# Four adjacency layers on one core: the first pass of layer 3 in the seven-product form too, and layer 2's chain laid out in half units

## The chip, the cores and the metric

The kernel runs on one NeuronCore of a Trainium2 chip, as one launch. The metric is the device time of that launch in microseconds. TensorE (PE in the profile) multiplies, VectorE (DVE), ScalarE (ACT) and GpSimd (POOL) do the elementwise work, and SyncE (SP) issues the DMAs. The median of three runs of the kernel before is 1045.57 us (1045.5 to 1046.95).

## The reference

Four layers share one 2048 x 2048 matrix `adj` (a sparse 0/1 pattern with a full diagonal, each row divided by its sum) and x of 8 batches x 2048 nodes x 64 channels. After each layer stands a residual and a layer norm. Cut to what matters:

```python
x = layernorm(x + L0(x, adj))        # x, A x and (2 A A - I) x, each by weights of its node
x = layernorm(x + L1(x, adj))        # attention over adj > 0.5
# layer 2
adj_i = adj + eye(N); deg = sum(adj_i, axis=1)
x = layernorm(x + (adj_i @ (x @ W.T + b)) / deg)
# layer 3: three passes, with node 0 set to intervention_value first
v = x.at[:, 0].set(intervention_value)
for _ in range(3):
    effects = adj @ v
    h = relu(concat([v, effects]) @ W1.T + b1)
    v = h @ W2.T + b2
x = layernorm(x + v)
```

## The kernel before

**Storage.** The 512 columns (8 batches x 64) form four chunks c = 0 to 3 of 128 columns. The 2048 nodes form four blocks j = 0 to 3 of 512 nodes. The pattern of `adj` lies in SBUF in fp8 (`Bm`, in the buffer `BW`), the row scales apart from it. Each moving operand x or v is held in `S` as a sum of two fp16 halves (high and low), so a product costs two matmuls for each of the 16 tiles of 128 nodes.

**Plain products.** A step P(k), k = 0 to 15, is layer 2's product for one (c, j): 32 matmuls of 512 columns in four pieces of 8 (`quarter`), and 8 of 128 columns with the diagonal. P(16) to P(31) are the first of layer 3's three passes: 32 matmuls of 512 columns and 3 more (`beside`), which add the part of W1 that multiplies v. The results go to the PSUM banks 0, 1, 2 in turn, and the step E(k) takes them out.

**Seven-product form.** The second and third pass take two chunks at once (n = 4 to 7; n // 2 is the pass, n % 2 the pair of chunks). Matrix and operand are cut into two by two blocks, and seven products of blocks do for eight, after a scheme of Winograd's kind. A product is a slot s = 0 to 6. Its operand is a block of v (X11, X12, X22) or a sum of blocks (S1 to S4). Its matrix block is a quarter of the pattern or a combination (T1 to T4, which GpSimd makes in the 64 steps `bt`). A slot is run in two half steps of 16 matmuls of 512 columns (jj = 0, 1). `V(n, s, jj)` takes a half step's bank out: ScalarE copies for s = 0 and 2, VectorE adds for s = 1, 3, 4, 5, and splits finished results into high and low half. `G` multiplies h by W2 and the adjacency weights, 12 matmuls of 128 columns. `mix` makes S1 to S4 on VectorE, `cut` splits an operand into its two halves, on ScalarE and then on GpSimd.

**Scales.** The fp16 halves need scales. For the second and third pass they are measured: VectorE takes the largest value of each block (a reduction to `gm` in `high`), a matmul (`gcol`) brings it across partitions, and the step `step` works out the next scale from it.

**Layer 2's chain.** Between P(4c+3) and layer 3's use of chunk c stands a chain over all engines, each step once for each j: W (TensorE by weights, then VectorE adds to X), `sq` (ScalarE) and `red` (VectorE) for the variance, `var`, a root on ScalarE, `rs` (five small VectorE instructions, the first of which is the reciprocal), `apply` (VectorE, X times 1/std), `v0t` and `v0` (ScalarE makes the high half of v in `S`, VectorE the low one), D (TensorE by the diagonal; ScalarE and VectorE split it into T), and G. `chk` and `sgn` (ScalarE, 16 each) check the matrix beside all this.

**Order.** Every engine runs one list in order, written out ahead by hand. `middle_order` lays the layers 0 and 1, `last_order` everything from P(1) on. In `last_order` a table puts each step ahead of a P(k) (one unit: about 8 us on TensorE) or a half step h of the seven-product part. All engines walk the same list and take from it what is theirs, and semaphores keep them apart. So the distance in the list between the maker and the user of a value is the time that it may take.

**Banks.** W, D, G, F take PSUM banks in rotation. `take_banks` works out for each such step, and for each half step that opens a bank (`pair_free`), what must have emptied that bank; TensorE waits for it. `D` on TensorE also waits for VectorE's last part of `v0` (`s_vl`). Lines of the steps: P L889, M L931, D L964, G L969, E on VectorE L1548, V on VectorE L1560, W on VectorE L1601, v0 L1620. In the profile the VectorE helpers `stt`, `ts`, `red` give L1224, L1216 or L1217, and L1227, apply is L1528, and mix L1600.

## Time and profile before

| | us |
|---|---|
| median of 3 runs | 1045.57 |
| profiled execution | 1046.92 |
| its span, first to last instruction | 1045.1 |
| TensorE busy | 1024.1 |
| VectorE busy | 692.9 |
| GpSimd busy | 534.7 |
| ScalarE busy | 453.1 |
| mean granted clock of TensorE | 0.995 of full |

The profile shows one execution. Its own time is 1.82 us above its span, and 1.35 us above the median. Busy time is time in which an engine has an instruction in work; matmuls overlap, so a matmul's mean duration is longer than the distance from one to the next. Layer 2 and the first pass of layer 3 lie between 525 and 792 us from the start of the span, the other two passes behind.

### The profile page before, as it was taken

How to read it: one execution, taken by the hardware profiler on the slowest of the kernel's cores; microseconds unless marked ns; L12 is line 12 of the kernel's file. 1: busy time of each engine (PE TensorE's matmuls, PEld its weight loads, DVE VectorE, ACT ScalarE, POOL GpSimd, SP SyncE). 2: the span in 40 equal slices, each digit the busy share in tenths (PEclk: the TensorE clock that was granted, in tenths of full speed). 3: DMA queues.
4: the chain of work that ended last, by engine and by line, in shares of the span. 5: the costliest groups of instructions: out<-in, count | busy, mean ns of one | idle time of the engine just before them, and what ended most of it. 6: DMA issues, size and time to landing. Idle time of an engine off the chain costs nothing.

```text
span 1045.1 us, 18762 instructions
## 1 busy us (share of the span) xinstructions
PE 1024.1 (98%) x6922; PEld 492.3 (47%) x6922; DVE 692.9 (66%) x1728; ACT 453.1 (43%) x1097; POOL 534.7 (51%) x625
## 2 busy tenths in 40 slices
PE   7999999999999999999999999999999999999995
PEld 3445444444444444434455555555554545455553
DVE  4877565656555886686577777875546676767556
ACT  4632323333334543444424667556557622141632
POOL 0005486644546686577645758579764233223311
PEclk9999999999999999999999999999999999999998
DMA  9930000000000000000010121112212100000022
GB/s 369 400 129 1 2 1 2 1 2 2 1 1 2 2 1 2 1 1 2 1 41 2 41 82 51 71 41 82 81 42 82 41 1 1 3 1 22 21 61 61
DMA packets 14658, 45.66 MB, mean 44 GB/s; under 512 B 960, under 2 KB 9280, under 8 KB 10080
## 3 DMA queue, kind: packets, MB, share of 16 engines
q1 hardware_dynamic: 14560, 44.39, 11.5%
q8 instruction: 57, 0.93, 0.4%
q14 instruction: 41, 0.34, 0.1%
HBM read 40.19 MB, written 4.19 MB: 42 GB/s over the span
## 4 chain that ended last, share of the span: by engine, by line
PE 95%; DVE 3%; ACT 1%; issue 0%; DMA 0%; SPq 0%; DVEq 0%; ACTq 0%
PE PS L771 37%; PE PS L901 23%; PE PS L945 18%; PE PS L823 5%; PE PS L756 2%; PE PS L758 2%; PE PS L757 2%; PE PS L765 1%; PE PS L764 1%; PE PS L763 1%; PE PS L746 1%; PE PS L926 1%; PE PS L747 1%; DVE X L1224 1%; DVE T L1224 0%; PE PS L809 0%
## 5 line engine op out<-in xcount | busy, mean ns | idle before, releaser
L771 PE MATMUL PS<-BW,S 128*128 128x512 fp8e4 x1792 | 403.2, 379 | 0.8 <-DVE R L1224 0.8
L771 PEld LDWEIGHTS PS<-BW,S 128*128 128x128 f16 x1792 | 169.9, 98 | 207.3 <-issue 16.6
L1064 ACT ACTIVATE T<-PS,SM 128x128 f32<-128x128 f32 x384 | 112.8, 365 | 234.5 <-DVE X L1224 157.2
L901 PE MATMUL PS<-WZ,R 64*128 64x512 f16 x1536 | 198.0, 377 | 1.7 <-ACT T L1064 1.7
L1768 POOL TENSOR_TENSOR T<-T 128x128 f32<-128x128 f32 (+1 forms) x192 | 124.3, 648 | 127.8 <-ACT T L1064 117.5
L1224 DVE SCALAR_TENSOR_TENSOR X<-PS,SM,X 128x128 f32<-128x128 f32 x320 | 110.0, 344 | 81.9 <-PE PS L901 81.9
L901 PEld LDWEIGHTS PS<-WZ,R 64*128 64x128 f16 x1536 | 69.5, 94 | 104.6 <-issue 26.3
L945 PE MATMUL PS<-BW,S 128*128 128x512 fp8e4 x512 | 115.4, 379 | 0.3 <-issue 0.3
L1224 DVE SCALAR_TENSOR_TENSOR T<-PS,SM,T 128x128 f32<-128x128 f32 x256 | 88.2, 344 | 28.9 <-PE PS L901 28.6
L1768 POOL TENSOR_TENSOR S<-R,S 128x512 f16<-128x512 f32 x48 | 57.5, 1210 | 93.5 <-ACT S L1064 93.5
L901 PE MATMUL PS<-WZ,T 64*128 64x512 f16 x768 | 103.8, 376 | 0.0
L1768 POOL TENSOR_TENSOR T<-R,T 128x512 f16<-128x512 f32 x42 | 49.6, 1187 | 75.4 <-DVE T L1216 52.7
L1790 POOL TENSOR_TENSOR BW<-BW 128x512 fp8e4<-128x512 fp8e4 x64 | 75.6, 1207 | 0.0
L945 PEld LDWEIGHTS PS<-BW,S 128*128 128x128 f16 x512 | 49.2, 98 | 55.7 <-issue 0.7
L1064 ACT ACTIVATE R<-PS,cs 128x512 f32<-128x512 f32 x48 | 32.7, 681 | 98.0 <-PE PS L765 68.7
L945 PE MATMUL PS<-BW,T 128*128 128x512 fp8e4 x320 | 72.8, 379 | 0.0
L1064 ACT ACTIVATE WZ<-WZ,ra 128x2048 f16<-128x2048 f32 (+1 forms) x32 | 63.9, 1996 | 0.5
L1768 POOL TENSOR_TENSOR X<-X,T 128x128 f32<-128x128 f32 x128 | 58.5, 457 | 10.0
L1216 DVE TENSOR_SCALAR T<-R 128x512 f16<-128x512 f32 x48 | 31.5, 657 | 47.5 <-ACT R L1064 46.6
L823 PE MATMUL PS<-BW,S 128*128 128x512 fp8e4 x240 | 54.9, 394 | 5.7 <-DVE BW L1221 5.7
L756 PE MATMUL PS<-hat,T 128*128 128x128 f16 x320 | 57.1, 220 | 2.4 <-DVE T L1224 2.4
L901 PEld LDWEIGHTS PS<-WZ,T 64*128 64x128 f16 x768 | 37.4, 94 | 45.5
(215 smaller groups left out, 1480.0 us busy)
## 6 DMA issues: line engine op xcount, KB each, us to landing
WZ<-a_in SPq DMA_DIRECT2D x16, 1024.0 KB, 4.8
BW<-at_in SPq DMA_DIRECT2D x8, 1024.0 KB, 18.5
R<-at_in SPq DMA_DIRECT2D x7, 1024.0 KB, 12.4
out<-X SPq DMA_DIRECT2D x16, 256.0 KB, 2.3
X<-x_in SPq DMA_DIRECT2D x3, 1024.0 KB, 19.9
T<-w_in SPq DMA_DIRECT2D x1, 1536.0 KB, 15.4
R<-at_in SPq DMA_DIRECT2D x2, 512.0 KB, 4.8
SM<-sm_in SPq DMA_DIRECT2D x1, 520.5 KB, 18.0
```

Of the source, the lines that this page charges most:

```text
L756: e.matmul(ok, th, hat[:, 0, kind, :], start=True, stop=False)
L757: e.matmul(ok, tl, hat[:, 0, kind, :], start=False, stop=False)
L758: m = e.matmul(ok, th, hat[:, 1, kind, :], start=False, stop=True)
L771: m = e.matmul(o, stile(h, t, c), Bm[:, t, block(j)], start=(t == 0 and h == 0), stop=(last and t == NT - 1 and h == 1))
L823: e.matmul(bank(2 * c + j), stile(h, jt, c), Bm[:, jt, block(j)], start=(jt == 0 and h == 0), stop=False)
L901: m = e.matmul(bank(b0 + q), halves[kd][zh][r, :], WZ[r, wh, kd, block(g)], start=(i == 0), stop=(i == 8))
L945: m = e.matmul(o, half_of(n, what, h, q % 2)[:, t, :], b[:, 4 * (q % 2) + t, :], start=(s in (0, 1, 3) and q % 2 == 0 and t == 0 and h == ...
L1064: return e.activation(o, i, f, **kw)
L1216: return e.tensor_scalar(o, i, s1, None, o1)
L1224: return e.scalar_tensor_tensor(out=o, in0=a, scalar=s, in1=b, op0=f, op1=g)
L1768: return e.tensor_tensor(o, a, b, f)
L1790: e.tensor_tensor(o, a, b, f, saturate=False).then_inc(s_bt, 1)
```

## The change

All three passes of layer 3 now have the seven-product form: n = 2 and 3 take the place of P(16) to P(31). The combinations of the matrix are needed earlier and in the order T3, T2, T1, T4, so GpSimd's `bt` steps start at P(1) and not at P(8). The scales of all passes are worked out beforehand from bounds, in `scales_b`; `gmax`, `gcol`, `step` and the reductions to `gm` are gone. Layer 2's chain is placed by half units y (a P(k) is two of them, y = 2k and 2k + 1; from y = 32 on y is the half step y - 32), and closer: D(c, 0) stands two half units behind `v0(c, 0)`, where it stood two units behind. The block E of the first pass is gone, with its VectorE and GpSimd parts. Some operands of n = 2 and 3 lie in a buffer in SM, and the squares of layer 2 in part of BW.

```diff
+BT_ORDER = ("T3", "T2", "T1", "T4")
...
-    return 16 * (p - 1) + (4 * c + j if p == 1 else 8 * (c // 2) + PAIR_UNITS.index((c % 2, j)))
+    return 16 * (p - 1) + 8 * (c // 2) + PAIR_UNITS.index((c % 2, j))
...
+    late, half, between = {}, {}, {}
+    def at(y, *steps):
+        (late if y < 32 else half).setdefault(y if y < 32 else y - 32, []).extend(steps)
+    def on(h, *steps):
+        half.setdefault(h, []).extend(steps)
 
     for k in sorted(after):
-        at(k, *after[k])
+        at(2 * k, *after[k])
     for c in range(NC):
         for j in range(4):
-            at(4 * c + j + 3, ("W", c, j))
-            at(4 * c + j + 4, ("sq", 2, c, j), ("red", 2, c, j))
-        k = 4 * c + 7
-        at(k, ("var", 2, c))
-        at(k + 1, ("rs", 2, c), ("apply", 2, c, 0), ("apply", 2, c, 1), ("v0t", c))
-        at(k + 2, ("apply", 2, c, 2), ("apply", 2, c, 3), ("v0", c, 0), ("v0", c, 1))
-        at(k + 3, ("v0", c, 2), ("v0", c, 3))
-        at(k + 4, ("D", c, 0), ("D", c, 1))
-        at(k + 5, ("D", c, 2), ("D", c, 3))
-        at(k + 6, ("G", 1, c, 0), ("G", 1, c, 1))
-        at(k + 7, ("G", 1, c, 2), ("G", 1, c, 3))
-    at(4, ("rows",))
+            y = 2 * (4 * c + j)
+            at(y + 4, ("W", c, j))
+            at(y + (5 if c == 3 else 6), ("sq", 2, c, j), ("red", 2, c, j))
+        y = 8 * c + (12 if c == 3 else 13)
+        at(y, ("var", 2, c))
+        at(y + 1, ("rs", 2, c), ("apply", 2, c, 0), ("apply", 2, c, 1), ("v0t", c))
+        at(y + 2, ("apply", 2, c, 2), ("apply", 2, c, 3), ("v0", c, 0), ("v0", c, 1))
+        at(y + 3, ("v0", c, 2), ("v0", c, 3))
+        at(y + 4, ("D", c, 0), ("D", c, 1))
+        at(y + 5, ("D", c, 2), ("D", c, 3))
+    at(8, ("rows",))
     for it in range(NT):
-        at(6 + 2 * it, ("chk", it))
-        at(7 + 2 * it, ("sgn", it))
-    at(24, ("gmax", 1, 0))
-    at(25, ("gcol", 1, 0), ("step", 1, 0))
-    at(27, *take(4, 0, "X11", "X12"))
-    at(28, cut(4, 0, "X11"), cut(4, 0, "X12"), *take(4, 0, "X21", "X22"))
-    at(29, *mixes(4, 0, 1, 3, 2), cut(4, 0, "X22"), cut(4, 0, "S2"), *mixes(4, 0, 4), *take(4, 1, "X11", "X22"))
-    at(30, cut(4, 0, "S1"), cut(4, 0, "S3"), cut(4, 0, "S4"), cut(4, 1, "X11"), cut(4, 1, "X22"), *take(4, 1, "X12", "X21"))
-    at(31, *mixes(4, 1, 1, 3, 2), cut(4, 1, "X12"), cut(4, 1, "S2"), *mixes(4, 1, 4))
+        at(12 + 4 * it if it < 5 else 32 + 4 * (it - 5) - (it - 5) // 4, ("chk", it))
+        at(14 + 4 * it if it < 5 else 34 + 4 * (it - 5) - (it - 5) // 4, ("sgn", it))
     for i in range(64):
-        at(8 + i // 3, ("bt", i))
-    for k in range(32):
-        order += late.pop(k, []) + (pieces("P", k) + [("E", k)] if k else [])
-    half = {}
-    def on(h, *steps):
-        half.setdefault(h, []).extend(steps)
-    for k in sorted(late):
-        on(2 * (k - 32), *late[k])
-    on(1, cut(4, 1, "S1"))
-    on(2, cut(4, 1, "S3"), cut(4, 1, "S4"))
-    for n in (5, 6, 7):
-        h, (p, g) = 14 * (n - 5), divmod(n - 2, 2)
-        on(h, ("gmax", p, g))
-        on(h + 2, ("gcol", p, g), ("step", p, g), *take(n, 0, "X11"))
+        at(2 + 4 * i // 7 if i < 56 else 38 + (i - 56) // 2, ("bt", i))
+    for n, y in ((2, 20), (3, 37)):
+        at(y, *take(n, 0, "X11", "X12"))
+        at(y + 1, cut(n, 0, "X11"), *take(n, 1, "X11", "X12"), cut(n, 0, "X12"))
+        at(y + 2, cut(n, 1, "X11"), cut(n, 1, "X12"))
+    for n, y in ((2, 28), (3, 43)):
+        at(y, *take(n, 0, "X21", "X22"))
+        at(y + 1, *mixes(n, 0, 1, 3, 2), cut(n, 0, "X22"), cut(n, 0, "S2"))
+        at(y + 2, cut(n, 0, "S3"), *mixes(n, 0, 4), *take(n, 1, "X22"), cut(n, 0, "S1"))
+        at(y + 3, cut(n, 0, "S4"), *take(n, 1, "X21"))
+        at(y + 4, *mixes(n, 1, 1, 3, 2), cut(n, 1, "X22"), cut(n, 1, "S2"))
+        at(y + 5, *mixes(n, 1, 4), cut(n, 1, "S1"))
+        at(y + 6, cut(n, 1, "S3"), cut(n, 1, "S4"))
+    for k in range(16):
+        p = pieces("P", k)
+        order += late.pop(2 * k, []) + (p[0:2] if k else []) + late.pop(2 * k + 1, []) + (p[2:4] + [("E", k)] if k else [])
+    for n in (4, 5, 6, 7):
+        h = 14 * (n - 3)
...
+    on(44, ("flags",))
+    on(46, ("total",))
+    on(47, ("verdict",))
...
-            n, s, jj = 4 + h // 14, h % 14 // 2, h % 2
+        if h < 84:
+            n, s, jj = 2 + h // 14, h % 14 // 2, h % 2
...
-        SQC = [flatR[:, 4096 + 512 * k:4608 + 512 * k] for k in range(2)] + [rowt[:, 512 * k:512 * k + 512] for k in range(2)]
+        SQC = [BW[:, NT * N + 28672 + 2048 * k:NT * N + 30720 + 2048 * k].bitcast(F32) for k in range(2)] + [rowt[:, 512 * k:512 * k + 512] for k in range(2)]
...
+        def made(n, jj, what):
+            return XB[:, 0 if what == "X11" else 1, :] if apart(n, jj, what) else MADE[what]
+        def apart(n, jj, what):
+            return n < 4 and jj == 1 and what in ("X11", "X12", "S4")
...
-                            for k in range(30, 32) if m == 4 else ():
-                                held[product_bank(k)] = (s_gt, k - 15)
-                            if m == 4:
-                                held[2] = (s_gt, 14)
+                            for k in range(13, 16) if m == 2 else ():
+                                held[product_bank(k)] = (s_zl, k + 1)
...
-                    if p == 0:
-                        e.wait_ge(s_sl, 4 * c + q + 1)
-                    else:
-                        e.wait_ge(s_ul, CN["G", p, c, q] + 1)
+                    e.wait_ge(s_sl, 4 * c + q + 1)
...
-                    if n == 4 and s == 2:
-                        e.wait_ge(s_bt, 64)
+                    if n == 2 and by[0] == "T":
+                        e.wait_ge(s_bt, NT * (1 + BT_ORDER.index(by)))
...
-                            m = beside(e, o, *ending(n, s, jj), 1, on=s > 1)
+                            m = beside(e, o, *ending(n, s, jj), min(n // 2 - 1, 1), on=s > 1)
...
-                elif kind == "gcol":
-                    p, g = step[1:]
-                    o = pe_aux(e, step)
-                    e.wait_ge(s_gmx, 2 * (p - 1) + g + 1)
-                    e.matmul(o[:, 0:128], gmh[:, g:g + 1].broadcast_to([128, 128]), i16[:, :], start=True,
-                             stop=True).then_inc(s_gmc, 1)
...
-                        fn(RT[k % 4], bank(product_bank(k)), ACT.Relu, scale=col(cKG0)).then_inc(s_gt, 1)
...
-                        e.wait_ge(s_p, 16 + 4 * block_of(n, jj, "X21" if what == "S4" else what)[0] + 4)
-                    fn(half_of(n, what, 0, jj), four(MADE[what]), ACT.Copy).then_inc(s_uh, 1)
+                        c, j = block_of(n, jj, "X21" if what == "S4" else what)
+                        e.wait_ge(s_d, 4 * c + j + 1)
+                    fn(half_of(n, what, 0, jj), four(made(n, jj, what)), ACT.Copy).then_inc(s_uh, 1)
...
-                fc(ts(e, col(cHB), col(cHB), 1e-10, qmax, ALU.max, ALU.mult))
-                fc(ts(e, col(cHB), col(cHB), 1.0 / 30000, None, ALU.mult))
-                fc(e.reciprocal(col(cT2), col(cHB)))
-                fc(ts(e, col(cKG0), col(cT2), col(cIRho), col(cT0), ALU.mult, ALU.mult))
-                fc(ts(e, cs[:, cSG:cSG + 4], ones[:, 0:4], col(cT2), None, ALU.mult))
-                fc(ts(e, cs[:, cISG:cISG + 4], ones[:, 0:4], col(cHB), None, ALU.mult))
+                fc(ts(e, col(cHB), col(cHB), 1e-10, None, ALU.max))
+                fc(e.tensor_tensor(col(cNMG), cs[:, cNG + 1:cNG + 2], cs[:, cNM + 1:cNM + 2], ALU.add))
+                fc(ts(e, col(cNMG), col(cNMG), 1e-3, None, ALU.max))
+                ip, sp, kp = ([col(k + p) for p in range(4)] for k in (cISG, cSG, cKG))
+                for p in (1, 2, 3):
+                    if p > 1:
+                        fc(stt(e, col(cHB), col(cHB), col(cNMG), col(cC1), ALU.mult, ALU.add))
+                    fc(ts(e, ip[p], col(cHB), qmax, 1.0 / (12000 if p < 3 else 60000), ALU.mult, ALU.mult))
+                    fc(e.reciprocal(sp[p], ip[p]))
+                    fc(ts(e, kp[p], sp[p], col(cIRho + min(p - 1, 1)), ip[p - 1] if p > 1 else col(cT0), ALU.mult, ALU.mult))
...
-            def high(f, c, j, n, largest):
-                hi = T[:, c, 0, block(j)]
-                ts(e, hi, f, 0.0, None, ALU.max).then_inc(s_gh, 1)
-                if largest:
-                    e.wait_ge(s_gh, n + 1)
-                    red(e, gm[:, c, j:j + 1], hi, ALU.max).then_inc(s_gm, 1)
...
+                ts(e, T[:, c, 0, block(j)], f, 0.0, None, ALU.max).then_inc(s_gh, 1)
...
-                        high(RT[k % 4], c, j, k - 16, True)
...
-                elif kind == "gmax":
-                    p, g = step[1:]
-                    e.wait_ge(s_gm, 16 * (p - 1) + 8 * g + 8)
-                    red(e, gmh[:, g:g + 1], gm[:, 2 * g:2 * g + 2, :].rearrange("p c j -> p (c j)"), ALU.max).then_inc(s_gmx, 1)
-                elif kind == "step":
-                    p, g = step[1:]
-                    sG, iG = cs[:, cSG + g:cSG + g + 1], cs[:, cISG + g:cISG + g + 1]
-                    n = 2 * (p - 1) + g + 1
-                    e.wait_ge(s_gmc, n)
-                    red(e, gmr[:, g:g + 1], bank(aux_bank["gcol", p, g])[:, 0:128], ALU.max).then_inc(s_gmr, 1)
-                    e.wait_ge(s_gmr, n)
-                    fc(e.tensor_tensor(col(cT0), gmr[:, g:g + 1], iG, ALU.mult))
-                    fc(e.tensor_tensor(col(cT1), col(cT0), col(cIQ), ALU.mult))
-                    fc(ts(e, col(cT1), col(cT1), col(cNG + 1), col(cC1), ALU.mult, ALU.add))
-                    fc(ts(e, col(cT1), col(cT1), fr[:, 1:2], None, ALU.mult))
-                    fc(stt(e, col(cT0), col(cT0), col(cNM + 1), col(cT1), ALU.mult, ALU.add))
-                    fc(ts(e, col(cT0), col(cT0), 1e-10, 1.0 / 15000, ALU.max, ALU.mult))
-                    fc(ts(e, CR[:, g, :], c1row[:, :], sG, col(cRho + 1), ALU.mult, ALU.mult))
-                    fc(e.reciprocal(sG, col(cT0)))
-                    fc(ts(e, cs[:, cKG + g:cKG + g + 1], sG, iG, col(cIRho + 1), ALU.mult, ALU.mult))
-                    e.tensor_copy(iG, col(cT0)).then_inc(s_kg, 1)
-                    e.wait_ge(s_kg, n)
...
+                    if k == 3 and q == 8:
+                        e.wait_ge(s_red, REDN[2, NC - 1, 3] + 1)
...
-                    add(T[:, c, 1, block(j)], RT[k % 4], T[:, c, 0, block(j)], ALU.subtract).then_inc(s_gl, 1)
```

What stands on the engines then, at the places that the prediction speaks of:

TensorE ahead of chunk 0's first D, before: P(10) ends (L926), and D (L746) follows it. The wait for s_vl is the one for `v0`.

```order
L771 MATMUL PS<-BW,S 128x512 [waits s_sl]
L771 MATMUL PS<-BW,S 128x512 x7
L771 MATMUL PS<-BW,S 128x512 [waits s_sl]
L771 MATMUL PS<-BW,S 128x512 x7
L926 MATMUL PS<-dg,S 128x128 x8
L746 MATMUL PS<-dg,S 128x128 [waits s_vl,s_y2]
```

TensorE after, at the same place: this is the middle of P(8), and its second half follows the two D.

```order
L769 MATMUL PS<-BW,S 128x512 [waits s_sl,s_zl]
L769 MATMUL PS<-BW,S 128x512 x7
L769 MATMUL PS<-BW,S 128x512 [waits s_sl]
L769 MATMUL PS<-BW,S 128x512 x7
L744 MATMUL PS<-dg,S 128x128 [waits s_vl,s_msum]
```

D(0, 0) has moved from behind P(10) into P(8), two and a half units earlier in TensorE's list.

VectorE ahead of layer 3, before, chunk 2's `apply` (L1528) and `v0` (S<-R and S<-X) with W(3, 2) (X<-PS) behind them:

```order
L1528 TENSOR_TENSOR X<-X,T 128x4x128 [waits s_rs] x2
L1224 SCALAR_TENSOR_TENSOR S<-R,cs,S 128x128 [waits s_vh]
L1224 SCALAR_TENSOR_TENSOR S<-X,cs,S 128x3x128
L1224 SCALAR_TENSOR_TENSOR S<-X,cs,S 128x4x128 [waits s_vh]
L1227 TENSOR_REDUCE T<-R 128x8 [waits s_sq]
L1224 SCALAR_TENSOR_TENSOR X<-PS,ra,X 128x128 [waits s_sc,s_bl,s_w]
L1224 SCALAR_TENSOR_TENSOR X<-PS,ra,X 128x128 x3
```

VectorE after, the same, from the second pair of `apply` to W(3, 2); R<-PS is a G, T<-PS is E(15):

```order
L1503 TENSOR_TENSOR X<-X,T 128x4x128 [waits s_rs] x2
L1198 SCALAR_TENSOR_TENSOR S<-R,cs,S 128x128 [waits s_vh]
L1198 SCALAR_TENSOR_TENSOR S<-X,cs,S 128x3x128
L1198 SCALAR_TENSOR_TENSOR S<-X,cs,S 128x4x128 [waits s_vh]
L1201 TENSOR_REDUCE T<-BW 128x8 [waits s_sq]
L1198 SCALAR_TENSOR_TENSOR R<-PS,ra,R 128x128 [waits s_ul,s_g]
L1198 SCALAR_TENSOR_TENSOR R<-PS,ra,R 128x128 x3
L1198 SCALAR_TENSOR_TENSOR T<-PS,T 128x512 [waits s_zh]
L1198 SCALAR_TENSOR_TENSOR S<-X,cs,S 128x4x128 [waits s_vh] x2
L1198 SCALAR_TENSOR_TENSOR X<-PS,ra,X 128x128 [waits s_sc,s_bl,s_w]
L1198 SCALAR_TENSOR_TENSOR X<-PS,ra,X 128x128 x3
```

All four `v0` of chunk 2 and E(15) now stand ahead of W(3, 2).

TensorE at the start of layer 3, before: a G or W (its last matmul is L758), and then P(16).

```order
L758 MATMUL PS<-hat,T 128x128
L771 MATMUL PS<-BW,S 128x512 [waits s_ul,s_zl]
L771 MATMUL PS<-BW,S 128x512 x7
L771 MATMUL PS<-BW,S 128x512 [waits s_ul]
```

TensorE after: W(3, 2) ends (L756), and the first half step of n = 2 follows, in the bank 4 that W(3, 2) has just written.

```order
L756 MATMUL PS<-hat,T 128x128
L936 MATMUL PS<-BW,S 128x512 [waits s_ul,s_y2]
L936 MATMUL PS<-BW,S 128x512 x7
L936 MATMUL PS<-BW,S 128x512 [waits s_ul]
L936 MATMUL PS<-BW,S 128x512 x7
L744 MATMUL PS<-dg,S 128x128 [waits s_vl,s_y2]
```

`s_y2` counts VectorE's W: the half step waits for VectorE's part of the W ahead of it (`held[4]` in `take_banks` is `(s_y2, 15)`, the fifteenth W).

## Rows read from the trace of the kernel before

**Rows 1.** The page's line of busy time, share and instructions.

```profile
PE 1024.1 (98%) x6922; PEld 492.3 (47%) x6922; DVE 692.9 (66%) x1728; ACT 453.1 (43%) x1097; POOL 534.7 (51%) x625
```

**Rows 2.** Page, chain that ended last: shares by engine.

```profile
PE 95%; DVE 3%; ACT 1%; issue 0%; DMA 0%; SPq 0%; DVEq 0%; ACTq 0%
```

**Rows 3.** Busy time by stretch: PE, PEld, DVE, ACT, POOL, clock, DMA, GB/s.

```profile
651.00:721.00 70.00, 70.00 (x470) 37.59 (x468) 57.74 (x102) 44.12 (x62) 50.73 (x42) 1.00 0.18 61
792.00:851.00 59.00, 59.00 (x347) 29.75 (x346) 40.05 (x83) 30.84 (x41) 19.44 (x16) 1.00 0.12 45
```

**Rows 4.** Chain in order of time: start, us, what; P(8) and P(9).

```profile
582.03 6.91 PE PS L771 x32
588.94 0.45 PE PS L926 x8
590.06 6.91 PE PS L771 x32
```

**Rows 5.** Groups, 514 to 911 us, by form: count, busy us, mean ns, idle before.

```profile
L1528 DVE TENSOR_TENSOR X<-X,T 128x512 f32<-128x512 f32 x28 | 29.0, 1075 | 0.2
L1224 DVE SCALAR_TENSOR_TENSOR T<-PS,T 128x512 f16<-128x512 f32 x32 | 20.9, 684 | 21.4 <-ACT T L1064 21.3
L1600 DVE TENSOR_TENSOR R<-R 128x512 f32<-128x512 f32 x24 | 19.5, 835 | 3.4 <-POOL S L1768 2.3
L1224 DVE SCALAR_TENSOR_TENSOR S<-X,cs,S 128x512 f16<-128x512 f32 x12 | 15.9, 1352 | 3.9 <-ACT S L1064 3.9
L1224 DVE SCALAR_TENSOR_TENSOR S<-X,cs,S 128x384 f16<-128x384 f32 x4 | 4.9, 1236 | 0.0
L1224 DVE SCALAR_TENSOR_TENSOR S<-R,cs,S 128x128 f16<-128x128 f32 x4 | 3.9, 969 | 0.0
L1224 DVE SCALAR_TENSOR_TENSOR R<-X,cs,R 128x128 f32<-128x128 f32 x4 | 2.2, 553 | 0.0
L1064 ACT ACTIVATE T<-PS 128x512 f16<-128x512 f32 x32 | 17.5, 586 | 13.0 <-PE PS L926 12.9
```

**Rows 6.** VectorE in order of time: start, us, instruction; chunks 0, 2 and 3.

```profile
576.83 3.46 DVE L1528 TENSOR_TENSOR X<-X,T 128x512 f32<-128x512 f32 x4
...
582.48 1.12 DVE L1224 SCALAR_TENSOR_TENSOR X<-PS,ra,X 128x128 f32<-128x128 f32 x4
...
653.38 0.34 DVE L1518 RECIPROCAL T<-T 128x32 f32<-128x32 f32 x1
...
655.72 1.29 DVE L1528 TENSOR_TENSOR X<-X,T 128x512 f32<-128x512 f32 x2
...
661.85 2.15 DVE L1224 SCALAR_TENSOR_TENSOR R<-PS,ra,R 128x128 f32<-128x128 f32 x8
663.91 3.06 DVE L1528 TENSOR_TENSOR X<-X,T 128x512 f32<-128x512 f32 x2
...
692.97 0.34 DVE L1518 RECIPROCAL T<-T 128x32 f32<-128x32 f32 x1
...
697.01 2.12 DVE L1528 TENSOR_TENSOR X<-X,T 128x512 f32<-128x512 f32 x2
```

**Rows 7.** GpSimd in order of time.

```profile
652.00 3.19 POOL L1790 TENSOR_TENSOR BW<-BW 128x512 fp8e4<-128x512 fp8e4 x3
661.29 1.16 POOL L1768 TENSOR_TENSOR T<-R,T 128x512 f16<-128x512 f32 x1 [6.11 <-DVE T L1216]
663.71 2.72 POOL L1768 TENSOR_TENSOR S<-R,S 128x512 f16<-128x512 f32 x2 [1.26 <-ACT S L1064]
```

**Rows 8.** TensorE in order of time: a gap near the end.

```profile
1035.36 0.22 PE L756 MATMUL PS<-hat,T 128*128 128x128 f16 x1 [2.06 <-DVE T L1224]
1035.41 0.22 PE L757 MATMUL PS<-hat,T 128*128 128x128 f16 x1
...
1035.94 0.31 PE L758 MATMUL PS<-hat,T 128*128 128x128 f16 x1
1036.05 0.31 PE L756 MATMUL PS<-hat,T 128*128 128x128 f16 x1
```

203 lines of the change are left out of this document (80 added, 123 removed).

## The prediction

> **What bounds the kernel now.** I read the line of busy time first: TensorE is busy for 1024.1 of 1045.1 us, VectorE for 692.9 [rows 1]. Then the chain that ended last: 95% of it is TensorE [rows 2]. So a matmul taken out counts in full, as long as no other engine makes TensorE wait for longer than that. Then the stretches, because a mean over the span hides where the others are near. From 651 to 721 us, at the start of layer 3, VectorE is busy for 57.74 of 70.00 us, though TensorE never waits there. Later, from 792 to 851 us, where n = 4 and 5 run, it is busy for 40.05 of 59.00 [rows 3]. The change puts the seven-product form into the first of these two stretches. That is why I follow VectorE's queue, and last look at single instructions in order of time [rows 6, 7].
>
> **What goes on TensorE.** P(16) to P(31) are 16 x 32 = 512 matmuls of 512 columns. The 28 half steps of n = 2 and 3 are 28 x 16 = 448. The 48 matmuls of `beside`, G, W and D stay. 32 such matmuls take 6.91 us, 0.216 us each [rows 4], so 64 fewer save 13.8 us. Four small matmuls of `gcol` go too. The trace shows no stall around them; I count 0.2 us. Gain: 14.0 us.
>
> **What it adds on VectorE.** The 16 blocks E of the first pass go with their reductions. V and `mix` for two n come: 16 mixes of 0.835 us alone are 13.4 us [rows 5]. V has three additions with splits and one addition for each n and jj, and that is more than E had. Of the 70 us from 651 on VectorE had 12.3 us free; the same work now has some 7 us less of TensorE time beside it. Layer 2's chain is drawn closer as well. A mean load near 1 is no wait in itself. What counts is where TensorE needs VectorE's newest result. I find four such places. Durations are the means of rows 5 where a row is named by kind; `rs` is five instructions from 653.38 to 655.72, 2.34 us; the four instructions of a W are 1.12 us, those of a G 2.15 / 2 = 1.07 us [rows 6]. A reduction of 512 elements is taken like VectorE's part of E, 0.68 us. TensorE's side is made of 6.91 us for 32 matmuls, 0.45 us for the eight with the diagonal, and 590.06 - 589.39 = 0.67 us for a W or G [rows 4].
>
> *Place 1, D(0, 0) and D(0, 1), now in the middle of P(8).* Before the change layer 1's last `apply` ends at 576.83 + 3.46 = 580.29 us [rows 6]. Now chunk 0's chain stands right behind it: rs 2.34, two apply 2.15, v0t 0.55, red 0.68, W 1.12, two apply 2.15, v0(0, 0) 0.97 + 1.24, v0(0, 1) 1.35. The sum is 12.55, so v0(0, 0) is there at 591.5 and v0(0, 1) at 592.8. P(8) starts at 582.03 [rows 4] plus one W more, and half of it is over at 586.2. TensorE waits for 5.3 us and then for 0.9 us: 6.2 us. If everything runs in 0.6 of its mean, as the pair of apply at 655.72 does (1.29 for 2.15), about 1 us is left. With rs at 4.04 (692.97 to 697.01) and pairs of apply at 3.06 [rows 6] it is 9.7.
>
> *Place 2, D(1, 0) and D(1, 1) in P(12).* Counted from the end of P(10): E(10) 0.59 + 0.68 on two engines, then the same 12.55: 13.8 us. TensorE has W, P(11), W, half of P(12) and D(1, 0) ahead of D(1, 1): 12.6 us. Wait: 1.2 us, from 0 to 5.
>
> *Place 3, the first half step of n = 2.* It takes bank 4, which W(3, 2) has written just ahead of it, so it waits for VectorE's part of W(3, 2) (`s_y2`). On VectorE that part stands behind nearly all of chunk 2's chain. From the end of P(14): E(14) 1.27, rs 2.34, two apply 2.15, v0t 0.55, W 1.12, mix 0.84, G 1.07, two apply 2.15, v0(2, 0) 2.21, v0(2, 1) 1.35, red 0.68, G 1.07, E(15) 0.68, two v0 2.70, W(3, 2) 1.12: 21.3 us. TensorE has four W or G and P(15), 2.7 + 7.4 = 10.0 us. Wait: 11.3 us. Even with VectorE free until P(15) ends, E(15), two v0 and W come behind it: 1.27 + 2.70 + 1.12 - 0.67 = 4.4 us. So 4 is the low end. With the slow durations of place 1 the high end is 15.5. Before the change no such wait was possible: P(16) took the bank of a product that had ended two units earlier.
>
> *Place 4, D(3, j) in n = 2.* Counted from the end of place 3's wait, VectorE has caught up. v0(3, 0) and G(1, 2, 3), whose banks D(3, 0) and D(3, 1) need, are ready within about 1 us of the time TensorE asks for them. I take 0, up to 5. The later half steps stand as n = 4 to 7 do, which ran with VectorE two thirds busy: 0.
>
> *The clock.* After a gap of 2.06 us near the end of the span the 128-column matmuls go from a distance of 0.05 us to 0.11 us [rows 8]: the granted clock falls from 2.4 to 1.2 GHz. Places 1 and 3 are longer gaps. How soon the clock comes back this trace doesn't show. If 16 matmuls of 512 columns run at half rate, 3.45 us are lost; if none, nothing. I take 1.5 us for each of the two gaps, 3.0 in all, between 0 and 6.9. The Trainium skill ("TensorE: Matmul & The Clock Gate", Part 1) says that the throttled state is the default and that sustained activity releases it, which speaks for a cost above zero at both gaps; by a rule that a warm array stays warm the term would be 0. The first half of it agrees with the row, the way back is shown by no row here.
>
> **Other edits.** `bt` starts earlier: 64 instructions, 56 of them beside layer 2. M with T2 needs 32, with T1 48, with T4 64 of them, and they stand two or more half steps ahead: no wait. `scales_b` has a few more one-column instructions at P(1), where VectorE has a slack of units. `chk` and `sgn` move on ScalarE, which was busy for 44.12 of 70 us. I cost these at nothing; ScalarE's and GpSimd's idle time hides them.
>
> **Sum.** Waits 6.2 + 1.2 + 11.3 + 0 + 3.0 = 21.7 us, gain 14.0 us, net +7.7 us. The profiled execution of 1046.92 us becomes 1054.6 us; it stood 1.35 us above the median, so the median goes from 1045.57 to 1053.3 us.
>
> **Rivals.**
> 1. *VectorE is quick, and the change is a gain.* The durations above are long because GpSimd works beside them. With GpSimd idle, from 655.19 to 661.29 us, two apply take 1.29 us; with it at work, from 663.71 on, 3.06 us [rows 6, 7]. If GpSimd has its pauses where the chain runs, the waits are 1 + 0 + 4 + 0, with no clock lost: 5 us against 14.0. Time: 1036.6 us. It decides at place 3: under a wait of some 6 us there, the sum of the waits stays under the gain. Against it: `bt` now stands in those pauses.
> 2. *GpSimd slows VectorE everywhere.* GpSimd was busy for 50.73 of 70 us already [rows 3], and 56 of the 64 `bt` now fall into the 16 units of layer 2, where 24 stood. With rs at 4.04 and pairs at 3.06 each time the waits are 9.7 + 4 + 15.5 + 3, with 5 for the clock: 37 us. Time: 1068.6 us. The Trainium skill ("GPSIMD Engine Reference", 1. Specifications) lists contention of GpSimd with VectorE instructions that have two SBUF inputs; by that rule every apply and v0 beside `bt` is slow, and the sum would be this one. The trace agrees for the pair at 663.91 us and shows that without GpSimd it is gone.
> 3. *The waits just eat the gain.* Places 1 and 3 at 4 and 8, 2 us elsewhere: 14 us, 1045.6 us.
> 4. *The change doesn't do what it says*, because the list makes TensorE wait for `cut` of n = 2, not for the bank. ScalarE and GpSimd finish those for X11 seven units ahead; S2 has five half steps. I give it nothing of its own; its price would be in 3.
>
> **How the numbers follow.** The forecast (some 4 us around the sum) has 0.48, rival 1 with its way to the forecast 0.27, rival 2 0.19, rival 3 0.06. A difference of 0.2%, 2.1 us, is about what can be told from none. Faster by more: 0.27; within: 0.06; slower: 0.67. The range from 1036 to 1064 us takes in rival 1 and the lower half of rival 2; the likeliest case's own range is 1048 to 1060.
>
> **What would show it.** Right: TensorE idle at the D of chunk 0 and ahead of the first half step of n = 2, with VectorE as releaser (5 and 11 us); a granted clock below 1 right behind; 64 fewer matmuls of 512 columns. Wrong: TensorE's chain without a gap between 525 and 800 us, or gaps that wait for GpSimd or ScalarE; VectorE's pairs of apply near 1.3 us there.

## The result and the profile after

The changed kernel takes 1071.05 us (median of 4 runs, 1070.51 to 1071.63), the kernel before 1045.53 on the same chip: the ratio is 1.024, with an interval from 1.0226 to 1.0254. The prediction said 1053.3, range 1036 to 1064. The direction was right, the size was not, and the time lies outside the range. The profiled execution's span is 1069.3 us; before it was 1045.1.

The page's line of busy time and the chain by engine of the changed kernel, beside [rows 1, 2]:

```profile
PE 1015.5 (95%) x6854; PEld 487.6 (46%) x6854; DVE 693.1 (65%) x1701; ACT 459.4 (43%) x1109; POOL 540.5 (51%) x625
```

```profile
PE 83%; DVE 8%; issue 4%; POOL 2%; ACT 2%; DMA 0%; SPq 0%; POOLq 0%; DVEq 0%; ACTq 0%
```

The 68 matmuls are gone (6922 to 6854). VectorE is as busy as before (693.1 against 692.9 us), but it now has 8% of the chain, and "issue" 4%. The waits themselves are TensorE's only gaps over 0.4 us from 500 to 760 us (start, duration, instruction, idle time before it and what ended it):

```profile
549.49 0.27 PE L754 MATMUL PS<-hat,T 128*128 128x128 f16 x1 [9.06 <-issue]
...
610.09 0.27 PE L744 MATMUL PS<-dg,S 128*128 128x128 f16 x1 [13.56 <-DVE S L1198]
...
611.59 0.26 PE L744 MATMUL PS<-dg,S 128*128 128x128 f16 x1 [0.49 <-DVE S L1198]
...
692.02 5.78 PE L936 MATMUL PS<-BW,S 128*128 128x512 fp8e4 x16 [9.65 <-DVE X L1198]
```

The reader is to see three places. The second and third are D(0, 0) with D(0, 1) and the first half step of n = 2, places 1 and 3 of the prediction. The first is W(0, 1) ahead of P(3), and the prediction doesn't have it. The profile names no releaser for that first wait ("issue"); what TensorE waited for is read from VectorE's rows below. The last row also shows the clock: its 16 matmuls of 512 columns take 5.78 us, and the next 16, with the clock up, take 3.62:

```profile
698.53 3.62 PE L936 MATMUL PS<-BW,S 128*128 128x512 fp8e4 x16
```

Busy time by stretch (PE, PEld, DVE, ACT, POOL, clock, DMA, GB/s), within the gaps and right after them:

```profile
540.00:550.00 10.00, 0.94 (x14) 0.79 (x12) 8.99 (x31) 0.00 (x0) 4.30 (x5) 0.64 0.00 1
550.00:560.00 10.00, 10.00 (x62) 5.37 (x61) 5.21 (x15) 2.83 (x5) 7.78 (x7) 0.85 0.01 2
600.00:610.00 10.00, 0.00 (x0) 0.00 (x0) 10.00 (x13) 5.39 (x10) 9.92 (x8) 0.54 0.27 105
610.00:613.00 3.00, 2.42 (x18) 1.91 (x19) 3.00 (x4) 1.66 (x4) 3.00 (x3) 0.50 0.04 8
692.00:695.00 3.00, 2.98 (x8) 1.05 (x9) 1.85 (x3) 0.63 (x1) 0.27 (x1) 0.50 0.00 0
```

From 600 to 610 us TensorE does nothing while VectorE is busy for all 10 us and GpSimd for 9.92. The sum: 1045.1 - 14.0 for the matmuls + 9.1 + 14.0 + 9.7 of waits makes 1063.9; the 5.4 us that are left to the measured 1069.3 I put down to the lower clock behind the three gaps. TensorE's busy time says the same: 1015.5 us, where 1024.1 - 14.0 would be 1010.1.

VectorE in order of time, ahead of the first wait. E(1)'s low half, which W(0, 1) needs, is the last row; it ends at 549.38, and W(0, 1) starts at 549.49:

```profile
539.09 1.02 DVE L1369 TENSOR_TENSOR cs<-cs 128x1 f32<-128x1 f32 x1
...
541.20 1.02 DVE L1198 SCALAR_TENSOR_TENSOR cs<-cs 128x1 f32<-128x1 f32 x1
542.25 1.02 DVE L1375 TENSOR_TENSOR cs<-cs 128x1 f32<-128x1 f32 x1
...
545.30 0.22 DVE L1198 SCALAR_TENSOR_TENSOR cs<-cs 128x1 f32<-128x1 f32 x1
...
548.69 0.69 DVE L1198 SCALAR_TENSOR_TENSOR T<-PS,T 128x512 f16<-128x512 f32 x1
```

GpSimd there:

```profile
540.06 4.25 POOL L1739 TENSOR_TENSOR BW<-BW 128x512 fp8e4<-128x512 fp8e4 x4
```

`scales_b` runs from 538.72 to 547.47 us, 8.75 us; before, it was done in 4.3 (539.29 to 543.63), and E(1)'s low half stood here:

```profile
544.86 0.69 DVE L1224 SCALAR_TENSOR_TENSOR T<-PS,T 128x512 f16<-128x512 f32 x1
```

Part of the growth is instructions, part is this: the same one-column instruction takes 1.02 us while GpSimd's four `bt` run (540.06 to 544.31) and 0.22 us a microsecond after them. (The first row's 1.02 us is no growth: it stands beside another GpSimd instruction and took 1.03 before, at 539.67.) And W(0, 1) stands one unit earlier than it did, so TensorE asked at 540.4 for what it had asked for at 548.2. Had E(1) been ready as early as before, at 545.55, TensorE would still have waited 5 us.

The chain between layer 1's last apply, which ends at 594.88, and D(0, 0):

```profile
595.17 0.88 DVE L1494 TENSOR_TENSOR T<-T 128x32 f32<-128x32 f32 x1
596.09 1.07 DVE L1495 TENSOR_TENSOR T<-T 128x32 f32<-128x32 f32 x1
597.20 1.29 DVE L1191 TENSOR_SCALAR T<-T 128x32 f32<-128x32 f32 x1
598.52 1.09 DVE L1497 TENSOR_TENSOR T<-T 128x32 f32<-128x32 f32 x1
599.65 2.36 DVE L1503 TENSOR_TENSOR X<-X,T 128x512 f32<-128x512 f32 x2
...
604.72 2.75 DVE L1503 TENSOR_TENSOR X<-X,T 128x512 f32<-128x512 f32 x2
607.39 1.18 DVE L1198 SCALAR_TENSOR_TENSOR S<-R,cs,S 128x128 f16<-128x128 f32 x1
608.49 2.95 DVE L1198 SCALAR_TENSOR_TENSOR S<-X,cs,S 128x384 f16<-128x384 f32 x2
```

These are the slow durations of the mean and above (rs 4.8 us, pairs of apply 2.36 and 2.75, against 3.06 at 663.91 in [rows 6]): 15.2 us to D(0, 0), where I had 11.2 to v0(0, 0).

### The profile page after: what moved, and what is told of

Same layout as the page of the kernel before. It is cut to its first block, busy times and chain, and to the rows that moved or that the text cites. A ratio compares the mean times of both kernels' runs of the same rounds, so it can differ in the third digit from the quotient of the medians.

```text
span 1069.3 us, 18663 instructions
## 1 busy us (share of the span) xinstructions
PE 1015.5 (95%) x6854; PEld 487.6 (46%) x6854; DVE 693.1 (65%) x1701; ACT 459.4 (43%) x1109; POOL 540.5 (51%) x625
## 3 DMA queue, kind: packets, MB, share of 16 engines
q1 hardware_dynamic: 14560, 44.39, 11.3%
## 4 chain that ended last, share of the span: by engine, by line
PE 83%; DVE 8%; issue 4%; POOL 2%; ACT 2%; DMA 0%; SPq 0%; POOLq 0%; DVEq 0%; ACTq 0%
PE PS L936 27%; PE PS L899 22%; PE PS L769 19%; PE PS L821 5%; PE PS L754 1%; PE PS L755 1%; PE PS L756 1%; DVE X L1503 1%; DVE R L1198 1%; PE PS L763 1%; PE PS L762 1%; PE PS L761 1%; DVE X L1198 1%; DVE S L1198 1%; DVE T L1198 1%
## 5 line engine op out<-in xcount | busy, mean ns | idle before, releaser
L769 PE MATMUL PS<-BW,S 128*128 128x512 fp8e4 x1280 | 293.0, 381 | 0.8 <-DVE R L1198 0.8
L769 PEld LDWEIGHTS PS<-BW,S 128*128 128x128 f16 x1280 | 120.8, 98 | 151.3 <-issue 19.9
L936 PE MATMUL PS<-BW,S 128*128 128x512 fp8e4 x768 | 175.3, 382 | 10.0 <-DVE X L1198 9.7
L936 PEld LDWEIGHTS PS<-BW,S 128*128 128x128 f16 x768 | 74.3, 99 | 95.0 <-DVE X L1198 9.8
L936 PE MATMUL PS<-BW,T 128*128 128x512 fp8e4 x480 | 109.3, 379 | 0.0
L1715 POOL TENSOR_TENSOR S<-R,S 128x512 f16<-128x512 f32 x42 | 50.3, 1204 | 110.9 <-ACT S L1049 110.9
L1198 DVE SCALAR_TENSOR_TENSOR R<-PS,cs,R 128x512 f32<-128x512 f32 x48 | 36.0, 750 | 78.6 <-PE PS L936 42.9
L936 PEld LDWEIGHTS PS<-BW,T 128*128 128x128 f16 x480 | 46.3, 98 | 52.9
L1198 DVE SCALAR_TENSOR_TENSOR R<-PS,ra,R 128x128 f32<-128x128 f32 x176 | 48.9, 341 | 24.8 <-PE PS L756 24.8
```

Of the source, the lines that this page charges most:

```text
L769: m = e.matmul(o, stile(h, t, c), Bm[:, t, block(j)], start=(t == 0 and h == 0), stop=(last and t == NT - 1 and h == 1))
L936: m = e.matmul(o, half_of(n, what, h, q % 2)[:, t, :], b[:, 4 * (q % 2) + t, :], start=(s in (0, 1, 3) and q % 2 == 0 and t == 0 and h == ...
L1198: return e.scalar_tensor_tensor(out=o, in0=a, scalar=s, in1=b, op0=f, op1=g)
L1715: return e.tensor_tensor(o, a, b, f)
```

## The experiments

"Waits" is the sum of TensorE's gaps over 0.25 us from 538 to 760 us in the profiled execution; the kernel before has none there, the changed one 32.8. The ratios are to the kernel before on the same chip (medians 1045.5 to 1046.3).

| edit on the changed kernel | us | ratio to before, interval | waits |
|---|---|---|---|
| none | 1071.05 | 1.024 [1.0226, 1.0254] | 32.8 |
| A1 `scales_b` later | 1070.68 | 1.0239 [1.0222, 1.0256] | 31.7 |
| A2 no `bt` in y = 8 to 12 | 1068.41 | 1.0214 [1.0197, 1.0231] | 27.8 |
| A3 no `bt` in y = 8 to 15 | 1066.83 | 1.0203 [1.0186, 1.022] | 28.5 |
| A4 W(3, 2) later | 1065.34 | 1.0188 [1.0171, 1.0205] | 26.9 |
| B1 D(0, j) later | 1068.07 | 1.0212 [1.0195, 1.0229] | 30.3 |
| B2 B1 and A1 | 1069.70 | 1.0219 [1.0202, 1.0236] | 31.8 |
| B3 B1, A4, chunk 2's D later | 1063.14 | 1.0154 [1.0137, 1.0171] | 26.5 |
| B4 B3, A1 and A3 | 1063.24 | 1.0163 [1.0146, 1.018] | 25.3 |
| C1 chunk 0's chain spread | 1067.95 | 1.0211 [1.0194, 1.0228] | 28.0 |
| C2 C1 and A1 | 1066.87 | 1.0204 [1.0187, 1.0221] | 25.4 |
| C3 chains of chunks 0, 2, 3 spread, A1, A3, A4 | 1059.72 | 1.0131 [1.0114, 1.0148] | 19.4 |
| D1 without `bt` | 1059.16 | 1.0128 [1.0109, 1.0146] | 19.9 |
| D2 C3, spread further | 1067.94 | 1.0212 [1.0195, 1.0229] | 23.2 |
| E1 C3 without `bt` | 1036.41 | 0.9915 [0.9898, 0.9931] | 4.5 |
| E2 C3, chunk 3's chain later | 1062.12 | 1.0157 [1.014, 1.0174] | 22.1 |
| F1 half of `bt` in layer 0 | 1063.35 | 1.0173 [1.0156, 1.019] | 24.8 |
| F2 C3 and F1, not A3 | 1043.25 | 0.9974 [0.9963, 0.9984] | 7.7 |

**A. One suspected place each.** My theory was that each wait is a place in the order, so that each goes when its place is mended.

```diff
-        at(2 * k, *after[k])
+        at(2 * k, *[x for x in after[k] if x != ("scales", 4)])       # A1
+    at(7, ("scales", 4))
...
-        at(2 + 4 * i // 7 if i < 56 else 38 + (i - 56) // 2, ("bt", i))
+        at(2 + i // 2 if i < 12 else 13 + (i - 12) * 24 // 43 if i < 56 else 38 + (i - 56) // 2, ("bt", i))   # A2
+        at(2 + i // 2 if i < 12 else 16 + (i - 12) // 2 if i < 56 else 38 + (i - 56) // 2, ("bt", i))         # A3
...
-            at(y + 4, ("W", c, j))
-            at(y + (5 if c == 3 else 6), ("sq", 2, c, j), ("red", 2, c, j))
+            late_w = (c, j) == (3, 2)                                    # A4
+            at(y + 4 + late_w, ("W", c, j))
+            at(y + (5 if c == 3 else 6) + late_w, ("sq", 2, c, j), ("red", 2, c, j))
```

A1: 

> The changed kernel with the scale chain scales_b moved from ahead of P(1) to half unit 7 (inside P(3)), nothing else. Theory: TensorE's new wait of 9.06 us at 540.42 us is W(0, 1), which needs E(1); E(1)'s low half stands on VectorE behind layer 1's chunk 3 and scales_b (538.72 to 547.47 us, 8.75 us). Without these E(1) is there at about 540, the wait falls to under 1 us, the slow clock behind it (P(2) or P(3) at 8.02 for 6.91 us, and its W) goes too: 10 to 11 us less, about 1060.5 us. Rival 1: the bank of W(0, 1), held by layer 0's last sums, is what comes late: no change, 1071 us. Rival 2: the time comes back at D(0, 0), whose wait of 13.6 us grows by what is saved, since chunk 3's layer 1 sets both: 1069 to 1071 us.

A2: 

> The changed kernel with no bt step in half units 8 to 12 (they follow from 13 on). Theory: four bt (574.66 to 578.98 us, 4.3 us) stand on GpSimd ahead of addrow, the last step of layer 1 that chunk 3's chain and so VectorE's queue wait for; D(0, 0)'s wait goes from 13.6 to 9 or 10 us, time about 1067 us. Rival: VectorE itself is slow beside GpSimd; addrow's place is no matter, the wait stays within 1 us of 13.6 and the time at 1070 to 1071 us.

A3: 

> The changed kernel with no bt step in half units 8 to 15, so that GpSimd runs none beside chunk 0's rs, apply and v0 either. Theory (GpSimd's bt costs twice): on top of e2 the chain from rs to v0(0, 0), 594.80 to 609.9 us, 15.1 us, goes to about 11; D(0, 0) waits 5 to 7 us; time about 1063 us. Rival: the chain's length isn't bt's doing (split stands beside it too): same as e2, within 1 us. The denser bt later may cost 1 or 2 us at n = 2.

A4: 

> The changed kernel with W(3, 2), its square and sum one half step later, so that the first half step of n = 2 takes a bank that G(1, 1, 2) held and VectorE emptied long before. Theory: the wait of 9.65 us for VectorE's part of W(3, 2) goes, and the slow clock behind it (5.78 for 3.45 us); D(2, 0) and D(2, 1) come next, and wait 1 to 4 us for v0. Time 1060 to 1063 us. Rival: VectorE is simply behind by 10 us there, and TensorE meets it at D(2, 0) or at the next bank: wait of 6 to 9 us, time 1068 to 1071 us.

A1 missed its 1060: 0.4 us less is nothing clear, and its rival 2 held. TensorE's largest gap in it:

```profile
608.43 0.26 PE L745 MATMUL PS<-dg,S 128*128 128x128 f16 x1 [15.77 <-DVE S L1199]
```

The wait at W(0, 1) fell from 9.06 to 2.64 us, three small ones at later W came up (3.1), and D(0, 0)'s grew from 13.56 to 15.77: TensorE arrived earlier at a place that VectorE's queue sets. A2 (1067 expected) came out near, A3 (1063 expected) 4 us above. D(0, 0) waits 9.37 and 8.04 us in them in place of 13.56, so some 4 us of it were `bt` ahead of `addrow`; what A3 frees beyond A2 comes back partly at 716 us (1.74). A4 gained 5.7 us, less than the 8 to 11 of the theory, and TensorE's gaps show what came instead:

```profile
687.61 0.22 PE L745 MATMUL PS<-dg,S 128*128 128x128 f16 x1 [0.96 <-DVE S L1199]
...
696.32 0.23 PE L745 MATMUL PS<-dg,S 128*128 128x128 f16 x1 [3.54 <-DVE T L1199]
```

**B. D(0, j) four half units later.** If the wait of 14 us is a matter of D's place, it goes.

```diff
+        y += (4, 0, 0, 0)[c]          # B1, B2; (4, 0, 1, 0) in B3, B4
         at(y + 4, ("D", c, 0), ("D", c, 1))
         at(y + 5, ("D", c, 2), ("D", c, 3))
...
-    for n, y in ((2, 20), (3, 37)):
+    for n, y in ((2, 24), (3, 37)):   # (3, 38) in B3, B4
```

B1: 

> Chunk 0's D four half units later (ahead of the halves of P(10) and P(11) in place of P(8)), its G with it; no other edit. Theory (the wait of 13.56 + 0.49 us is a matter of the place: VectorE has work without a gap from the end of layer 1's norm to D, 15 us for which the order leaves 3.45): both waits go, and the clock's share behind them (1.9): 1071.05 - 14.05 - 1.9 = 1055, 1053 to 1059 with small waits at chunk 1's D, where chunk 0's G now stands too; the wait of 9.65 before the half step of n = 2 stays, since VectorE idles half of 620 to 640. Rival (VectorE is behind for good): the wait of n = 2 grows by what the other lost, 1066 to 1071.

B2: 

> The same, and scales_b from y = 2 to y = 7. By itself scales_b's move was worth 0.4 us, since what W(0,1) no longer waited (9.06 to 2.64, and 3.1 at three later W) came back at D(0,0) (13.56 to 15.76), which VectorE's chain set. Theory: with D(0,0) later nothing stands behind that chain, so that the same move is now worth 9.06 - 5.75 = 3.3 and 1 of the clock: 4 us less than the kernel with the late D alone, 1049 to 1053. Rival (the move is worth nothing as such): as the late D alone, within 1 us.

B3: 

> Chunk 0's D four half units later, and at chunk 2 W(3,2) one half step later and D and G one half unit later. Theory: the late D's 1055, less the wait of 9.65 and its clock (2.3); with W(3,2) alone moved 4.5 came back as waits of D(2,0) and D(2,2), and one half unit is 3.9: 1043 to 1048. Rival (VectorE's work for n = 2 is the bound at 660 to 694, wherever the instruction stands that waits): 5.7 less than the late D alone and no more, 1049 to 1050.

B4: 

> All four at once: chunk 0's D late, scales_b at y = 7, no bt in y = 8 to 15, W(3,2) later with chunk 2's D and G one half unit later. Theory (every wait is one of place; VectorE's work fits in the time as a whole): what is left is 1 to 6 of small waits on the after's 1036: 1038 to 1044, below the kernel before. Rival (VectorE is the bound from 538 to 694 as a whole): 1048 or more.

The theory fell. B1 gained 3 us, not 16. D waits no more, but a W does, in TensorE's order:

```profile
612.56 0.27 PE L755 MATMUL PS<-hat,T 128*128 128x128 f16 x1 [11.19 <-issue]
```

and VectorE's gives the reason: the low half that is this W's input (the last row below, 611.78) runs behind all applies and the first two v0 of chunk 0. By the lists it is E(7)'s, and the W is W(1, 3); the expectation of C1 below names them E(8) and W(1, 2).

```profile
607.81 1.18 DVE L1199 SCALAR_TENSOR_TENSOR S<-R,cs,S 128x128 f16<-128x128 f32 x1
608.91 2.95 DVE L1199 SCALAR_TENSOR_TENSOR S<-X,cs,S 128x384 f16<-128x384 f32 x2
611.78 0.68 DVE L1199 SCALAR_TENSOR_TENSOR T<-PS,T 128x512 f16<-128x512 f32 x1
```

D was only the first to ask. B2 and B4 show the same: what A1 and A3 free is waited for elsewhere. B3's 4.9 us under B1 is A4's gain again, near its rival's 5.7.

**C. The chains spread.** New theory: VectorE's queue is in order, and rs to v0 of a chunk, 15 us, stand in three half units of 3.45 us. C1 gives chunk 0's applies and v0 the half units 16, 18 and 20, as before the change; C3 also spreads chunks 2 and 3 and takes in A1, A3 and A4. The operands of the first pass follow: `take` of n = 2 from y = 24, in C3 that of n = 3 from y = 39 and 45.

```diff
-        y = 8 * c + (12 if c == 3 else 13)
-        at(y, ("var", 2, c))
-        at(y + 1, ("rs", 2, c), ("apply", 2, c, 0), ("apply", 2, c, 1), ("v0t", c))
+        y = ((15, 16, 18, 20, 21, 22), (21, 22, 23, 24, 25, 26), (30, 31, 33, 34, 36, 37), (36, 37, 39, 40, 41, 42))[c]  # C3
+        at(y[0], ("var", 2, c))
+        at(y[1], ("rs", 2, c), ("apply", 2, c, 0), ("apply", 2, c, 1), ("v0t", c))
...
```

C1: 

> Chunk 0's chain of layer 2 at the spacing that it had in the kernel before: rs, two applies and v0t at y = 16, two applies and two v0 at 18, two v0 at 20, D at 21 and 22, G from 24. The late D alone left 11.2 us of the wait: TensorE stood before W(1,2), whose input E(8) low ran on VectorE at 611.78, behind all of chunk 0's applies and v0 (595.38 to 611.7). Theory (VectorE's queue in its order: the chain's 15 us stand ahead of the next low halves, and only spreading it lets them by): the wait of 11.2 falls to at most 4, since each piece is now 4 to 6.5 us and a full unit of TensorE is 7: 1068.07 - 7 to 11 - 1.5 of the clock = 1055 to 1060. Rival (VectorE's sum of work from 538 on is what is late, not its order): under 3 us less than the late D, 1065 or more.

C2: 

> The same, and scales_b at y = 7. So far this move gained nothing (with the late D 1069.7 against 1068.1), because VectorE had no free time between E(1) and chunk 0's chain for what it was moved to. Theory: if the spread chain gives that time, 3 us less than the spread chain alone, 1052 to 1057. Rival (it only passes the wait on): as the spread chain alone, within 1 us.

C3: 

> Chunk 0's chain as in the two others, scales_b at y = 7, no bt in y = 8 to 15, W(3,2) a half step later, and the chains of chunks 2 and 3 spread too (applies and v0 of chunk 2 at 31, 33, 34, D 36 and 37, G 39; of chunk 3 37, 39, 40, D 41 and 42, G 45). With all of this but the spreading it took 1063.2, with waits of 2.65, 11.55, 1.54 and 9.54 us, the last behind chunk 2's and n = 2's work on VectorE. Theory (order): 11.55 to at most 4, 9.54 to at most 5: 1063.2 - 12 - 2.5 of the clock = 1049, 1043 to 1052. Rival (VectorE's sum of work bounds the stretch): 1058 or more.

C1 missed too. The 11.19 us at the W became 1.19 us, but four small waits at D and W follow, and one of 4.28 at 642 us, where chunk 1's chain now meets chunk 0's D and G on VectorE's list. C2 took 1.1 us less than C1, its rival's value, not its theory's. C3 gained 11.3 us and kept 19.4 of waits, the two largest these:

```profile
634.63 0.29 PE L756 MATMUL PS<-hat,T 128*128 128x128 f16 x1 [4.27 <-DVE X L1200]
...
715.50 0.29 PE L756 MATMUL PS<-hat,T 128*128 128x128 f16 x1 [7.49 <-DVE R L1200]
```

VectorE was busy for the whole of both waits (4.20 of 4.20 us from 630.4, 7.50 of 7.50 from 708.0), GpSimd for all of the first and for 2.94 us of the second. So the next runs took GpSimd's part away.

**D and E. Without `bt`, and spread further.**

```diff
-        at(2 + 4 * i // 7 if i < 56 else 38 + (i - 56) // 2, ("bt", i))
+        pass                                            # D1, E1
...
-                return BT[:, i - 1, :, block(jj)]
+                return Bm[:, 8 * (i // 3):8 * (i // 3) + 8, block(2 * (i % 2) + jj)]
```

D1 and E1 leave out the 64 `bt` and TensorE's wait for them, so they don't compute the layer; they only tell what `bt` costs. D2 changes C3's table to D(0, j) at 22 and 23, chunk 1 at 22, 24, 25 with D at 27, chunk 3 at 38, 40, 41 with D at 42, and the first G of each later; E2 only chunk 3's row to (36, 38, 40, 41, 42, 43).

D1: 

> The changed kernel without the 64 bt on GpSimd (T1 to T4 aren't computed; the products read quarters of B in their place, so the number and form of the matmuls stay). Theory (the order bunches VectorE's work; its own durations matter less): VectorE's chain from layer 1's last apply to D(0,0), 15.1 us, keeps its slow applies beside split and addrow, and W(0,1)'s wait has no bt in it: the wait at D(0,0) falls by the 4.7 us that the addrow came earlier without bt and by 2 to 3 of the chain (as with no bt in y = 8 to 15: 8.0 was left), the wait of 9.65 by at most 2: 1062 to 1067. Rival (contention with bt on GpSimd is what makes VectorE late): VectorE's 1.0 to 1.5 us applies and v0 go to 0.7 everywhere, some 15 us in the stretch, and the waits with them: 1045 to 1055.

D2: 

> As the kernel with everything spread, further: chunk 0's D at 22 and 23 and G from 26, chunk 1's applies and v0 at 22, 24, 25, D at 27 and 28, G from 29, chunk 2's G from 40, chunk 3's applies and v0 at 38, 40, 41, D at 42 and 43, G from 46. Left over there: 2.65 (W(0,1)), 1.2 + 1.1 + 0.5 (chunk 0), 4.3 (W(2,1), behind chunk 1's v0 and chunk 0's G on VectorE), 1.5 + 0.7, 7.5 (G(1,2,1), whose bank waits for G(1,2,0)'s sum behind chunk 3's chain on VectorE). Theory (order): 4.3 and 7.5 go with 2.5 of the clock: 1059.7 - 12 to 14 = 1046 to 1049. Rival (sum of work): the same waits somewhere later, 1056 to 1060.

E1: 

> The spread order (chunk 0's, 2's and 3's chains apart, scales_b at y = 7, W(3,2) a half step later) without the 64 bt on GpSimd (T1 to T4 aren't computed; the products read quarters of B). Theory (contention with bt and the bunched order each make VectorE late, by themselves): the gains of 11.9 and 11.3 add up to most of their sum, so 1071.05 - 18 to 22 = 1049 to 1053, with waits of 5 to 12 us in all. Rival (both gave VectorE the same time back, so that the second is worth little): 1056 to 1059.

E2: 

> As the kernel with everything spread, and chunk 3's rs, applies and v0 one half unit later again (38, 40, 41, D 42 and 43), so that on VectorE chunk 2's first two G stand ahead of chunk 3's second applies. Theory (a place in the order): the 7.5 us before G(1,2,1) and 1.5 of the clock go, at most 3 come back at chunk 3's D: 1059.7 - 6 to 9 = 1051 to 1054. Rival (VectorE has no free time there, so that its sum of work is the bound): within 2 us of 1059.7.

D1, 1059.16 us, fell between its theory (from 1062) and its rival (to 1055), so neither the order nor the contention is the whole. D1's waits are 6.51, 6.23 and 7.13 us at the three places of the changed kernel. VectorE in time in it:

```profile
541.85 0.22 DVE L1196 SCALAR_TENSOR_TENSOR cs<-cs 128x1 f32<-128x1 f32 x1
542.10 0.16 DVE L1373 TENSOR_TENSOR cs<-cs 128x1 f32<-128x1 f32 x1
...
592.75 3.25 DVE L1501 TENSOR_TENSOR X<-X,T 128x512 f32<-128x512 f32 x2
...
598.71 1.28 DVE L1501 TENSOR_TENSOR X<-X,T 128x512 f32<-128x512 f32 x2
599.91 0.34 DVE L1196 SCALAR_TENSOR_TENSOR S<-R,cs,S 128x128 f16<-128x128 f32 x1
600.17 1.27 DVE L1196 SCALAR_TENSOR_TENSOR S<-X,cs,S 128x384 f16<-128x384 f32 x2
```

Apart from the third row, the same instructions that took 1.02, 1.02, 2.75, 1.18 and 2.95 us take 0.22, 0.16, 1.28, 0.34 and 1.27. The third row, the first pair of apply, is slower still, 3.25 us for 2.36: it runs beside GpSimd's other work (587.06 to 598.35), so `bt` isn't all that slows VectorE.

E1 shows that it takes both. It took 1036.41 us, 34.6 us less than the changed kernel, where the order alone (C3) gave 11.3 and leaving out `bt` alone (D1) 11.9. The gains do more than add up, so its theory (1049 to 1053) was too careful and its rival wrong. The stretch from 538 to 720 us in E1 (same columns as the windows above):

```profile
538.00:720.00 182.00, 177.52 (x1256) 98.15 (x1255) 140.51 (x326) 111.65 (x163) 72.58 (x56) 1.00 0.14 47
```

and in C3, with `bt`:

```profile
538.00:720.00 182.00, 162.48 (x1109) 89.02 (x1108) 154.44 (x303) 100.84 (x150) 138.18 (x112) 0.95 0.12 41
```

C3's VectorE spends 154.44 us on 303 instructions, E1's 140.51 us on 326, so E1's gets further in less busy time: 85% of the stretch in C3, 77% in E1. Leaving out `bt` takes two things away, its place in GpSimd's queue and what it does to VectorE. The pages show the second by itself. VectorE is busy for 693.1 us in the changed kernel and 673.6 in D1, for 699.5 in C3 and 672.1 in E1, with the same 1701 instructions: `bt` costs VectorE 19.5 us of its own time in the one order and 27.4 in the other. Of the place in GpSimd's queue, A2 shows 4.2 us at D(0, 0). TensorE's busy time has a share too: 1018.3 us in C3, 1009.3 in E1. Behind C3's wait of 7.49 us, 16 matmuls of 512 columns took 5.7 us again, so I put these 9.0 us down to the clock; with 16 us fewer gaps in the whole span they make up the 25.0 between the two spans.

That a wait moves on to the next asker while VectorE's queue is this full, and is gone once it has room, is how I read B, C and E1 together. No run shows at which load the one becomes the other: in the changed kernel, held up as it is, VectorE is busy for 77% of the same stretch too.

D2 and E2 fell. In D2 the waits of 4.27 and 7.49 us that C3 had went or moved, but the one of 1.47 at 696 us grew to 4.43, and new ones came: 8.45 us at chunk 3's D (725.58) and 3.56 at 771. E2's waits at 711 and 730 us, 4.83 and 3.82, replace C3's 7.49. Both are slower than C3: two more rounds at places alone gained nothing while `bt` was there.

**F. `bt` elsewhere.** T3 and T2 are made from the pattern alone (T2 by way of T3). The first 32 `bt` go into layer 0's stage, one beside each of 32 of its 64 steps; there, from 300 to 538 us, GpSimd was busy for 160.7 of 238 us.

```diff
+    spots = [2, 4, 6, 8, 9] + list(range(10, 16)) + [16 * k + g for k in (1, 2, 3) for g in (0, 1, 6, 8, 9, 10, 15)]
+    for i in range(32):
+        at(spots[i], ("bt", i))
...
-    for i in range(64):
-        at(2 + 4 * i // 7 if i < 56 else 38 + (i - 56) // 2, ("bt", i))
+    for i in range(32, 64):
+        at(14 + 5 * (i - 32) // 6 if i < 56 else 38 + (i - 56) // 2, ("bt", i))
```

F1: 

> The changed kernel with bt 0 to 31 moved into layer 0's stage (one beside each of 32 of its 64 steps), 32 to 55 over y = 14 to 33; the rest as it was. Theory (bt beside layer 1's and 2's chains slows VectorE): as without bt up to 590 us, half of the slowing after it: the waits of 23 before 612 fall to 14 to 16, W(3,2)'s stays at 8 to 10: 1061 to 1064, if layer 0's stage hides 32 x 1.2 = 39 us of GpSimd (its idle time there is 84). Rival (GpSimd in layer 0's stage holds the adds and so TensorE): the gain is lost there, 1068 to 1080.

F2: 

> The spread order (chunk 0's, 2's and 3's chains apart, scales_b at y = 7, W(3,2) a half step later) with the same early bt. Theory: between the spread order with bt (1059.7) and without it (1036.4), nearer to the second since only 32 of the 64 are left beside the chains and those later: 1040 to 1048, so faster than the kernel before or level with it. Rival (bt in layer 0's stage holds up TensorE there, or half of bt beside the chains is enough to make VectorE late): 1052 to 1065.

Both theories held: 1063.35 (1061 to 1064 expected) and 1043.25 us (1040 to 1048). F2 leaves nothing out and is the only whole kernel here that is faster than the one before, by 0.3%: 0.9974 of it, interval 0.9963 to 0.9984; its 8 runs (up to 1044.08) all lie under the 11 of the kernel before (from 1045.01). TensorE's gaps from 300 to 538 us are 2.3 us, as before, so layer 0's stage hides the 32 `bt` wholly. VectorE is busy for 685.0 us in all, between C3's 699.5 and E1's 672.1. F2's page and stretch:

```profile
PE 1012.4 (97%) x6854; PEld 486.3 (47%) x6854; DVE 685.0 (66%) x1701; ACT 459.8 (44%) x1109; POOL 540.0 (52%) x625
```

```profile
538.00:720.00 182.00, 174.16 (x1205) 95.52 (x1204) 148.43 (x317) 110.53 (x162) 109.61 (x87) 0.98 0.13 47
```

## Why the prediction was wrong, step by step

- *The gain of 14.0 us*: right. TensorE is busy for 1009.3 us in E1, 14.8 less than before. E1 has 3.5 us more gaps over 0.25 us than before in its whole span; 1045.1 - 14.0 + 3.5 is 1034.6, and its span is 1033.8.
- *`scales_b`, "a few more one-column instructions at P(1), where VectorE has a slack of units", costed at nothing*: this step failed, and it cost 9.1 us. It is the only wait of which the prediction has nothing. I took the slack from the order before, in which W(0, 1) stood a unit later, and even there it was 2.6 us (E(1) ready at 545.55, W at 548.19). The earlier W makes 5 of the 9.06 us; `scales_b` took 8.75 in place of 4.3 us, and that is the rest. D1's wait of 6.51 at this place says that 2.5 us of this growth are `bt`'s; A1 says that all but 2.6 of the 9.06 need `scales_b` there.
- *Place 1, 6.2 us*: the mechanism was right, the size was not: 14.05 us. Of the 7.9 us missing some 4 are `bt` ahead of `addrow` on GpSimd (A2: 9.37 left of 13.56), which I had under "Other edits" at nothing, since I only asked who waits for `bt` and not what stands behind it. The other 4 are the chain's durations, 15.2 us in place of 11.2; without `bt` (D1) it still takes 11.9. The prediction also read the place too narrowly: B1 shows that E(7)'s low half is behind the same queue.
- *Place 2, 1.2 us*: no wait. TensorE came to D(1, 1) 12.6 us after the end of P(10), as the sum had it, but the chain was done after 11.2 (at 648.14 us) and not 13.8. rs took 1.24 us and each pair of apply 1.3. GpSimd was idle from 636.79 to 642.98, beside all of rs and the first pair, which is the mechanism of rival 1; the second pair was as quick at the start of GpSimd's next work:

```profile
639.66 1.29 DVE L1503 TENSOR_TENSOR X<-X,T 128x512 f32<-128x512 f32 x2
...
642.77 1.28 DVE L1503 TENSOR_TENSOR X<-X,T 128x512 f32<-128x512 f32 x2
```

- *Place 3, 11.3 us*: right in its mechanism and near in size, 9.65 us, by the instruction named. (Its high end of 15.5 doesn't follow from the rows: the slow rs and pairs add 3.5 to 11.3, which is 14.8.)
- *Place 4 and the later half steps, 0*: right (0.35 us at 934.68 us, GpSimd's).
- *The clock, 3.0 us for two gaps*: 5.4 for three, 1.8 each where I had 1.5. The row of the half step shows 2.2 us for its 16 matmuls.
- *The range*: it ended at 1064 because I gave rival 2, with 1068.6 us, only its lower half. Its mechanism, VectorE slow beside GpSimd, is real (19.5 us of VectorE's time, by D1) but doesn't hold everywhere: from 612 to 720 us an apply takes 0.69 us in the mean. That its waits and clock, 37 us, come near the measured 38.2 is luck: it has 4, 15.5 and 3 us at places 2 to 4, where 0, 9.65 and 0 were measured, and nothing at W(0, 1). I put its chance at 0.19 although [rows 6, 7] showed the pair of apply at 3.06 us beside GpSimd and the change put 32 more `bt` into the stretch.

Not settled is how the 34.6 us divide between the order and `bt`: by themselves they are 11.3 and 11.9, together more, and what one is worth depends on the other. C3's 11.3 also has A3's later `bt` in it. Nor is it settled how much of `bt`'s part on TensorE is GpSimd's queue and how much VectorE's slower instructions.

## What to carry to other kernels

A wait of the engine that sets the time is set by the whole queue ahead of what it waits for. Before mending its place, ask who next asks that queue; if the queue is full there, as VectorE's was for 21.5 of the 22 us from 590 to 612, moving the asker only passes the wait on (B1: 16 us expected, 3 had). Moved "hidden" work must be priced by what stands behind it on its own engine and by what it slows on its neighbour: the 64 `bt`, whose results nobody waited for, cost 12 us where they stood, 23 us once the order was spread, and their first half cost nothing in layer 0's stage.

## What the runs showed of the hardware

Beside a busy GpSimd not all VectorE instructions slow down. Those with two SBUF tensors do, whatever their size: the 128x1 ones go from 0.16 to 1.02 us, applies of 128x512 from 0.69 up to 1.5 or 1.6. So do tensor_scalar instructions with one SBUF tensor of 32 columns at times (1.29 us in the chain's rows above, 0.18 at the same place in D1), but not those of one column (0.15). Reductions (0.68 us) and those with one input in PSUM (E's low half 0.68, W's 0.34 each) don't, in the profiles read here. That a one-column instruction takes a whole microsecond looks like waiting for a GpSimd instruction (1.06 us each there, 4.25 for four) to end. The Trainium skill ("SBUF — State Buffer", Who interferes with whom) describes it as an exclusive lock held for the full instruction, not a shared bandwidth; the trace fits that: 0.16 us stretched to 1.02 is near the length of one GpSimd instruction. No run here tests it further.
